# The row of maxima goes into the scores' operand without waiting for GpSimd's part of that operand; the first scores wait for both

## The reference, cut to what matters

```
q = x @ Wq.T + bq                    # 16 heads of depth 8
k = context @ Wk.T + bk
v = context @ Wv.T + bv
scores = einsum('bhtd,bhcd->bhtc', q, k) / sqrt(d)
attn = softmax(scores, axis=-1)
out = einsum('bhtc,bhcd->bhtd', attn, v)
x = x + tanh(g_xattn) * (out @ Wo.T + bo)       # attention on layernorm(x)
x = x + tanh(g_ffn) * experts(layernorm(x))     # top 8 of 160, and a shared one
```

## Time and profile before

| | |
|---|---|
| median of 3 runs (lowest to highest) | 1141.21 us (1140.9 to 1142.85) |
| profiled execution, its own time | 1140.58 us |
| its span in the trace | 1139.1 us |
| busy PE, DVE, ACT, POOL | 1069.6, 969.8, 845.1, 610.7 us |

### The profile page before, as it was taken

One profiled execution on the slowest core, in us unless ns is written; L12 is line 12 of the kernel. 1 busy time (PEld: TensorE's weight loads), 2 busy tenths in 40 slices (PEclk: granted clock), 3 DMA queues, 4 the chain that ended last, 5 costly groups with the idle time before them and its releaser, 6 DMA issues.

```text
span 1139.1 us, 37969 instructions
## 1 busy us (share of the span) xinstructions
PE 1069.6 (94%) x12090; PEld 708.6 (62%) x12090; DVE 969.8 (85%) x1706; ACT 845.1 (74%) x1812; POOL 610.7 (54%) x1042
## 2 busy tenths in 40 slices
PE   2798899999999999999999999879999999999998
PEld 1366677777777777777777777644555555555554
DVE  3677788888888888888888888669999999999998
ACT  2566577777777777767777776658888888888886
POOL 4887888888888888888888988000000000000000
PEclk9799999999999999999999999889999999999999
DMA  6786866757667767568577552146777767776673
GB/s 129 162 179 150 187 155 171 170 137 182 154 143 184 156 161 176 135 159 180 139 182 164 132 144 61 25 138 209 231 226 232 239 227 226 234 236 226 225 240 115
DMA packets 201816, 197.06 MB, mean 173 GB/s; under 512 B 161999, under 2 KB 168207, under 8 KB 201782
## 3 DMA queue, kind: packets, MB, share of 16 engines
q1 hardware_dynamic: 188292, 174.14, 58.2%
q0 software_dynamic: 11520, 20.99, 6.5%
q10 hardware_dynamic: 1970, 1.49, 0.7%
HBM read 109.96 MB, written 12.55 MB: 108 GB/s over the span
## 4 chain that ended last, share of the span: by engine, by line
PE 45%; POOL 21%; issue 16%; DVE 9%; SPq 3%; DMA 2%; POOLq 2%; ACT 1%; DVEq 0%; ACTq 0%
PE bank L1368 15%; PE bank L1340 15%; PE bank L1170 4%; PE bank L1184 4%; DVE part_max L897 3%; POOL ctx_parts L495 3%; PE bank L1203 3%; POOL q_st L603 3%; POOL q_blk L585 3%; POOL w_in L468 3%; POOL w_in L470 2%; POOL w_out L516 2%; POOL w_out L515 2%; DVE rec L1024 2%; PE bank L1239 2%
## 5 line engine op out<-in xcount | busy, mean ns | idle before, releaser
L701 ACT ACTIVATE p_exp<-bank 125x448 f32<-125x448 f32 x768 | 400.2, 544 | 193.4 <-PE bank L1184 192.4
L897 DVE TENSOR_REDUCE part_max<-bank 128x1 f32<-128x500 f32 x672 | 420.9, 672 | 71.6 <-PE bank L1203 71.2
L1184 PE MATMUL bank<-q_st,k_stk 97*125 97x224 f16 x1536 | 275.6, 264 | 15.5 <-DMA q_st<-neg_row 8.9
L1203 PE MATMUL bank<-kparts,q_blk 128*128 128x500 f16 x672 | 256.3, 385 | 13.4 <-DVE part_max L897 11.2
L1184 PEld LDWEIGHTS bank<-q_st,k_stk 97*125 97x125 f16 x1536 | 197.2, 139 | 80.3 <-ACT p_exp L701 16.4
L1368 PE MATMUL bank<-ctT,w_ring 128*128 128x448 f16 x960 | 234.0, 353 | 3.0 <-DVE ctT L1072 3.0
L778 ACT ACTIVATE ctT<-bank 128x448 f32<-128x448 f32 x320 | 173.6, 543 | 40.6 <-PE bank L1340 16.1
L1072 DVE TENSOR_TENSOR ctT<-k_stk,ctT 128x448 f16<-128x448 f32 x320 | 198.2, 619 | 0.5 <-ACT ctT L784 0.4
L1170 PE MATMUL bank<-p_exp,v_sb 125*25 125x168 f32 (+1 forms) x6144 | 187.9, 263 | 0.4 <-ACT p_exp L701 0.4
L784 ACT ACTIVATE ctT<-k_stk 128x448 f16<-128x448 f32 x320 | 181.7, 568 | 5.5 <-DVE k_stk L1066 3.2
L1340 PE MATMUL bank<-q_hi,w_ring 128*128 128x448 f16 x640 | 174.0, 354 | 2.4 <-ACT k_stk L767 2.4
(11 more groups left out here) (157 smaller groups left out, 1241.1 us busy)
## 6 DMA issues: line engine op xcount, KB each, us to landing
v_sb<-c_scratch SPq DMA_DIRECT2D x114, 448.0 KB, 4.0
k_stk<-kparts SPq DMA_DIRECT2D x384, 93.8 KB, 3.5
ctx_in<-in_ctx_dram SPq DMA_DIRECT2D x30, 672.0 KB
k_stk<-c_scratch SPq DMA_DIRECT2D x38, 448.0 KB, 3.9
w_scratch<-w_out POOLq DMA_DIRECT2D x80, 128.0 KB, 3.2
w_in<-in_L_ffn_w_gate_dram POOLq DMA_DIRECT2D x160, 32.0 KB, 3.3
w_in<-in_L_ffn_w_down_dram POOLq DMA_DIRECT2D x80, 64.0 KB, 3.4
ctx_in<-in_ctx_dram SPq DMA_DIRECT2D x30, 78.0 KB
```

The costliest lines, as they stand in the source:

```text
L701: act.activation(p_exp[0:KP, j % PR, f * 448:(f + 1) * 448], ST[f][0:KP, 0:448], ACT.Exp).then_inc(exp_done, 1)
L897: v.reduce_max(part_max[:, i // NCH, i % NCH:i % NCH + 1], SM[i % NSM][:, 0:CK], axis=AX.X).then_inc(sm_maxed, 1)
L1184: last = pe.matmul(ST[f][0:KP, (g % 2) * GC:(g % 2 + 1) * GC], k_stk[0:97, u, g, j * KP:(j + 1) * KP], q_st[0:97, u, g, :, :].rearrange("p ...
L1203: pe.matmul(SM[i % NSM][:, 0:CK], rows, kparts[:, u, 0, c * CK:(c + 1) * CK], start=True, stop=True).then_inc(sm_done, 1)
```

## The change

SP's wait for `qst_made` ahead of the row's DMA is taken out. PE waits for `qst_made` itself, once a batch, ahead of the batch's first scores, where it waits for `kst_here` and `row_here` already:

```diff
@@ -400,7 +400,6 @@
                 if on(step, 1):
                     u = back(step, 1)[1]
                     b = num(back(step, 1))
-                    sp.wait_ge(qst_made, b + 1)
                     sp.wait_ge(neg_copied, b + 1)
                     sp.dma_start(q_st[96:97, u, :, :, :].rearrange("p a b c -> p (a b c)"), neg_row[:, :])\
                       .then_inc(row_here[u], 16)
@@ -1178,6 +1177,7 @@
                 b = num(bt)
                 if j == 0 and f == 0:
                     pe.wait_ge(kst_here[u], h * (16 * 3 * HG) + 16 * 3 * HG)
+                    pe.wait_ge(qst_made, b + 1)
                     pe.wait_ge(row_here[u], h * 16 + 16)
                 until(pe, exp_done, b * (2 * KT) + (2 * j + f - 1))
```

## The result

The changed kernel took 1144.0 us (median; 1142.25 to 1149.36) against 1141.32 of the kernel before in the same comparison (1138.23 to 1145.25): ratio 1.0026, 95% interval [1.0018, 1.0035]. The forecast was no change, 1141.1 within 1138.8 to 1143.1. The kernel is slower, and the time lies outside the range.

The account below looks back on a forecast made before the run. POOL was taken to set the pace from about 106 to 700 us. A 2.0 us lead of TensorE, nearly all lost at POOL's layernorm, left 0.1 to 0.2 us of gain: 1141.1 us, range 1138.8 to 1143.1.

Parts of the forecast that it names:

- The added wait costs nothing: One more semaphore at TensorE ahead of 32 first scores, taken at nothing; without the lead's cover, 1 us.
- Row transfer off the path: At batch 21 the row lands before POOL is done; 2.08 us between POOL and PE become 0.1, gaining 2.0.
- The lead is earned once and taken back at the tokens: PE's 2.0 us lead, gained at batch 3, ends in step 32 waiting for POOL's xc; 0.1 or 0.2 us left.
- same: Outcome that the measurement can't tell from no change, about 0.2% or 2.3 us; chance 0.82.
- The clock at 132 us: Low TensorE clock after batch 3's 3.03 us wait, 1.7 us of work, forecast gone but worth nothing at the end.
- POOL runs freely from 106 us: POOL waits for no other engine until about 700 us; rival, off its pace by a microsecond or more: 0.10.
- The new wait cools TensorE: Rival: the 1.8 us wait for xc in step 32 lowers the clock, 1142.8 us, or 1146 if long; chance 0.08.
- Everything is earned: Rival: POOL follows PE, so waits and clock give 6.2 us in all, 1135.0 us; chance 0.05.

Follow-up runs that it names:

- pe_wait_only: Kernel before with only TensorE's added wait for qst_made, SP's wait for POOL kept: 1142.95 us, ratio 1.0026.
- after_rec_psum: Changed kernel with DVE's reciprocal written in place in PSUM, so o_nrm reads one SBUF operand: 1142.66 us, ratio 1.0024.
- before_again: Kernel before, unchanged, measured and profiled a second time: 1140.2 us, ratio 0.9997.
- one_sem: Changed kernel with POOL counting on the row's own semaphore, so TensorE's program has its old 1844 instructions: 1142.19 us, ratio 1.0004.
- after_pe_pad76: Changed kernel with 76 more idle instructions at the start of TensorE's stream (1924 in all): 1143.46 us, ratio 1.0014.
- one_sem_rec_tokens: one_sem with the reciprocal in place in PSUM and the tokens' transposes one slot later in step 32: 1138.04 us, ratio 0.9971.
- after_again: Changed kernel, unchanged, measured and profiled a second time: 1146.31 us, ratio 1.0056.
- one_sem_rec: one_sem with the reciprocal written in place in PSUM: 1140.86 us, ratio 0.9996.

## Why the prediction was wrong

- **The added wait costs nothing: wrong, and this is the step that failed.** It looked at what TensorE does while it waits, and there it does cost nothing (41.34 to 41.35 us for two steps in pe_wait_only, as before). It didn't ask where the four instructions push the rest of the program. Inside the loop and always fulfilled the wait measured 1.0026, four idle instructions at the start of the kernel before 1.0017, and the changed kernel with the old length 1.0004. What the runs show in place of "nothing" is a block of TensorE's program that is fetched among SP's six issues: these take 0.7 to 1.0 us more, and TensorE waits 1.2 to 1.5 us longer at L1368 in four of the five profiles (0.6 in after_rec_psum). That the fetch delays the issues is shown by moving it; how it does so isn't. The sum should have held these 1.2 to 1.5 us. The ratios say 2 to 3 us, and where the rest comes from stays open. A part may be the lower clock behind the longer wait, 1.4 us in the changed kernel's first profile: from L1368 to the end it is 1.0 us more on average. But before_again has the lower clock and 368.2 us there with short issues, so this isn't shown. And with the fetch moved away the changed kernel measured 1.0004 [0.9991, 1.0017] in one_sem but 1.0014 [1.0001, 1.0028] in after_pe_pad76, so that a part of the loss may not be the fetch's.
- **Row transfer off the path: right at batch 21** (0.18 us between POOL and TensorE; forecast 0.1), wrong at batches 3 and 20. At batch 3 the transfer was sized by batch 21's row (1.82 to 2.05 us), which had left with the DMA engines 1% busy; with the engines 94% busy it took 4.22 us. The fixed cost of about 2.0 us that I took from the Trainium skill ("DMA: Bandwidth & Descriptors", Anatomy of one DMA) is given there for DMAs that GpSimd issues, and SP issues this one; the traces agree with it in the quiet cases only. At the end this changed nothing that can be seen, as the lead over POOL was there at batch 29.
- **The lead is earned once and taken back at the tokens: right.** 1.75 us of lead at batch 29 (2.0), a wait of 1.49 us for `xc` at L1103 (1.5 to 2). one_sem, which shows the change without the shifted fetch, ends at 1.0004, the "same" that was forecast; after_pe_pad76, which shows it too, at 1.0014. That it is this wait which takes the lead back fits both and isn't shown by itself, as said at one_sem_rec_tokens.
- **The clock at 132 us:** forecast as gone; as TensorE waited 3.18 us there, it came back (0.60 over 132 to 136 us, before 0.57), and with it no gain.
- **POOL runs freely from 106 us: wrong in size.** No engine made it wait, but DVE lengthened its instructions: 1.6 us of drift up to batch 29 (a rival, up to 3.4 us). Whether that costs time at the end isn't settled. In one comparison the kernel without it is faster (after_again to after_rec_psum, 1146.31 to 1142.66 us), but against the first measurement of the changed kernel it isn't (1.0026 and 1.0024), and with the fetch at its old place the two intervals overlap (1.0004 and 0.9996).
- **The new wait cools TensorE:** it did in after_again and in one_sem_rec (1.7 and 1.6 us), as that rival had it, and not in five other profiles with a wait of 1.4 us or more at this place. Forecast at 0.08, the low clock is real in two of seven. That it costs time at the end isn't shown: the six issues begin at 766.15 us in one_sem_rec, with the low clock, and at 766.19 in one_sem_rec_tokens, without it.
- **Everything is earned: no.** With both additions it is 0.9971, and without the change they alone give 0.9984. The range ended at 1143.1, so a loss by the fetch of 1.2 to 1.5 us alone would still have been inside it; that it holds so much is width, not foresight.

## What to carry to other kernels

An edit that adds or removes instructions on an engine moves its later code against the borders of the blocks in which the program is fetched, here by four instructions out of some 1850. When the time moves in a stage that the edit doesn't touch, look in that stage for transfers of kind "instruction", and repeat the measurement with a few idle instructions at the start, in the kernel before as well as in the changed one. A wait that is taken out can also have held a transfer back until the DMA engines were idle, so look at how busy they are at the new time. Where two engines run side by side for hundreds of us, a new distance between them can lock them into meeting at every second turn. And where one kernel, measured twice, differs by 0.3%, an effect of 0.1 to 0.2% needs both kernels in the same comparison, several times.

## What the runs showed of the hardware

- A fetch of TensorE's program that falls among SP's six DMA issues lengthens them by 0.7 to 1.0 us, in five profiles of five, and in none of the other twelve.
- DVE's product with two SBUF operands and POOL's cast lengthen each other by 0.16 and 0.17 us when they meet. With the reciprocal left in PSUM (one_sem_rec) the product's mean over 300 to 660 us is 391 ns:

```profile
L1027 DVE TENSOR_TENSOR o_nrm<-bank,o_raw 128x224 f32<-128x224 f32 x18 | 7.0, 391 | 0.6
```

and in the changed kernel 527, in the kernel before 459:

```profile
L1027 DVE TENSOR_TENSOR o_nrm<-rec,o_raw 128x224 f32<-128x224 f32 x17 | 9.0, 527 | 0.6
```

```profile
L1028 DVE TENSOR_TENSOR o_nrm<-rec,o_raw 128x224 f32<-128x224 f32 x17 | 7.8, 459 | 0.6
```

  So some products are longer in the kernel before as well, though only 2 of its casts are; after_again has 471 ns.

- A row of 1.8 KB lands 1.82 us after its issue with the DMA engines 1% busy (506.04 us before) or 34% busy (103.41 us after), after 1.90 us at 69%, and after 4.22 us at 94% (4.79 in after_again, at 102% by the same measure).
- 252 instructions that do nothing but wait for semaphores already fulfilled took TensorE some 28 us, 0.11 us each.
- Behind the wait at L1368 the granted clock isn't the same in all executions of one kernel: over 764 to 776 us it is 1.00 in one profile of the kernel before and 0.86 in the other, and from L1368 to the end they take 366.7 and 368.2 us. Single profiles scatter as much as the effects here are large.
